# Another order of the six deep layers' queues, on all five engines of one core

## The reference

```
for i in range(DEPTH):                      # DEPTH = 6
    x = attn_layer(shift_tokens(x), Wqkv[i], q_scale[i], k_scale[i], Wo[i]) + x
    x = ffn_layer(shift_tokens(x), ln_g[i], ln_b[i], W1[i], b1[i], W2[i], b2[i]) + x
```

## Time and profile before

| | us |
|---|---|
| median of 3 runs (3456.48 to 3460.31) | 3459.82 |
| the profiled execution, its own time | 3457.47 |
| its span, first to last instruction | 3455.5 |
| TensorE busy | 3392.5 (98%) |
| VectorE busy | 3123.3 (90%) |
| ScalarE busy | 3047.1 (88%) |
| GpSimd busy | 2706.0 (78%) |

### The profile page before, as it was taken

How to read it: one execution, slowest core, us unless ns; L and a number is a source line. 1 busy time by engine, 2 the same in 40 slices (tenths; PEclk the granted TensorE clock), 3 DMA queues, 4 the chain that set the end, 5 groups by cost and what they waited for, 6 DMA issues and landing times.

```text
span 3455.5 us, 109160 instructions
## 1 busy us (share of the span) xinstructions
PE 3392.5 (98%) x43104; PEld 2518.0 (73%) x43104; DVE 3123.3 (90%) x4897; ACT 3047.1 (88%) x5393; POOL 2706.0 (78%) x2652
## 2 busy tenths in 40 slices
PE   8998899999999999999999999999999999999998
PEld 6885677777777777777777777777777777777776
DVE  6886999999999999999999999999999999989994
ACT  5665799999999999999999999999999999999996
POOL 3434888888888888888887888888888888888782
PEclk9998999999999999999999999999999999999999
DMA  1001212212211221221221221222122222122111
GB/s 44 27 3 46 56 39 58 68 39 53 55 49 48 68 52 40 55 58 39 67 52 43 52 58 47 59 52 52 43 58 55 51 52 52 38 74 52 37 50 42
DMA packets 61704, 171.33 MB, mean 50 GB/s; under 512 B 9488, under 2 KB 21392, under 8 KB 60816
## 3 DMA queue, kind: packets, MB, share of 16 engines
q1 hardware_dynamic: 61200, 164.36, 18.7%
HBM read 21.72 MB, written 4.19 MB: 8 GB/s over the span
## 4 chain that ended last, share of the span: by engine, by line
PE 88%; DVE 4%; DMA 3%; issue 2%; POOL 2%; ACT 1%; SPq 1%; DVEq 0%; POOLq 0%; ACTq 0%
PE bank L1021 11%; PE bank L1037 10%; PE bank L1002 9%; PE bank L969 9%; PE bank L986 8%; PE bank L1361 7%; PE bank L920 7%; PE bank L922 6%; PE bank L921 6%; PE bank L1374 3%; DMA vbuf<-v_stage 3%; PE bank L380 2%; PE bank L360 2%; PE bank L1346 2%; PE bank L345 2%
## 5 line engine op out<-in xcount | busy, mean ns | idle before, releaser
L1286 POOL TENSOR_TENSOR rotbuf<-mbuf 128x512 f32<-128x512 f32 x768 | 982.1, 1284 | 318.2 <-PE bank L969 308.5
L1300 POOL TENSOR_TENSOR rotbuf<-rotbuf,rs 128x512 f32<-128x512 f32 x768 | 793.8, 1044 | 7.5
L1173 DVE TENSOR_TENSOR mbuf<-bank,table 128x512 f32<-128x512 f32 x768 | 526.6, 686 | 100.4 <-ACT sq L1063 99.8
L1310 POOL TENSOR_TENSOR probs<-probs,rden 128x768 f32<-128x768 f32 x384 | 566.9, 1476 | 35.8 <-DVE rden L1252 28.5
L1063 ACT ACTIVATE sq<-bank 128x512 f32<-128x512 f32 x768 | 461.9, 601 | 71.0 <-PE bank L922 55.1
L1174 DVE TENSOR_TENSOR mbuf<-bank,table 128x512 f32<-128x512 f32 x768 | 522.3, 680 | 0.0
L969 PE MATMUL bank<-ident,rotbuf 128*128 128x128 f32 x3072 | 468.6, 275 | 7.7 <-DVE mbuf L1174 5.4
L969 PEld LDWEIGHTS bank<-ident,rotbuf 128*128 128x128 f32 x3072 | 365.9, 141 | 135.1 <-ACT qbuf L1083 18.1
L1155 DVE TENSOR_REDUCE ss<-sq 128x16 f32<-128x1024 f32 x384 | 461.3, 1201 | 0.2 <-issue 0.2
L920 PE MATMUL bank<-weights,inputs 128*128 128x512 bf16 x1152 | 444.6, 386 | 15.5 <-DVE mbuf L1174 11.8
L1021 PEld LDWEIGHTS bank<-probs_t,vbuf 96*64 96x64 f32 x12288 | 389.3, 138 | 96.3 <-issue 94.4
(11 more groups left out here) (115 smaller groups left out, 6269.2 us busy)
## 6 DMA issues: line engine op xcount, KB each, us to landing
vbuf<-v_stage SPq DMA_DIRECT2D x192, 384.0 KB, 4.5
vbuf<-v_stage SPq DMA_DIRECT2D x192, 256.0 KB, 3.5
vbuf<-v_stage SPq DMA_DIRECT2D x96, 128.0 KB, 4.5
stage<-in_wqkv SPq DMA_DIRECT2D x36, 256.0 KB, 5.0
weights<-in_wo SPq DMA_DIRECT2D x6, 512.0 KB, 6.3
out_t<-weights SPq DMA_DIRECT2D x1, 2048.0 KB, 6.3
weights<-out_t SPq DMA_DIRECT2D x1, 2048.0 KB, 10.6
out_t<-weights SPq DMA_DIRECT2D x16, 128.0 KB, 2.2
```

The costliest lines, as they stand in the source:

```text
L1173: e.tensor_tensor(b.m1[:, u % 2, :].rearrange("p (h s d) -> p h s d", h=8, s=2), pj, cos, ALU.mult)
L1286: e.tensor_tensor(b.rot[:, u, :], b.m1[:, u % 2, :], b.m2[:, u % 2, :], ALU.add).then_inc(s.rotated, 1)
L1300: e.tensor_tensor(v, v, r, ALU.mult).then_inc(s.scaled, 1)
L1310: e.tensor_tensor(probs, probs, b.rden[:, p % 2, :].unsqueeze(2).broadcast_to([P, 8, BLOCK_K]), ALU.mult).then_inc(s.probs, 1)
```

## The change

Nothing is computed differently and no step is added or dropped: each engine's slot holds the same steps in another order, many with another instance number, and the ring of the three shared banks follows TensorE's new order. The head of the diff:

```
 WORK_RING = (
-    ("up", 1, -3), ("pj", 5, 1), ("t", 4, 0), ("pj", 6, 1), ("up", 2, -3), ("t", 5, 0), ("t", 6, 0),
...
+    ("v", 2, 0), ("t", 0, 0), ("pj", 2, 1), ("out", 0, -2), ("t", 1, 0), ("t", 2, 0), ("pj", 3, 1),
+    ("up", 0, -3), ("t", 3, 0), ("up", 1, -3), ("v", 3, 0), ("up", 2, -3), ("pj", 4, 1), ("pj", 5, 1),
+    ("t", 4, 0), ("t", 5, 0), ("pj", 6, 1), ("mu", 0, -2), ("pj", 7, 1), ("dn", 0, -3), ("t", 6, 0),
+    ("t", 7, 0), ("v", 0, 1), ("v", 1, 1), ("pj", 0, 2), ("pj", 1, 2),
 )
 PE_REACH = (-3, 2)
-ACT_REACH = (-4, 2)
+ACT_REACH = (-3, 2)
 DVE_REACH = (-6, 2)
-POOL_REACH = (-2, 2)
-SP_REACH = (1, 1)
+POOL_REACH = (0, 2)
+SP_REACH = (0, 1)
```

```
+    act_copy_t(e, s, b, at, 1, 1)
+    act_ff_shift(e, s, b, at, -1)
+    act_square(e, s, b, at, 2, 3)
...
+    act_copy_t(e, s, b, at, 0, 2)
+    act_ff_gelu(e, s, b, at, -3, 0)
+    act_copy_pt_of(e, s, b, at, -1, 1)
+    act_copy_t(e, s, b, at, 0, 3)
+    act_ff_gelu(e, s, b, at, -3, 1)
     act_copy_v(e, s, b, at, 0, 3)
...
+    act_input_of(e, s, b, at, 2)
+    act_ff_gelu(e, s, b, at, -3, 2)
+    act_square(e, s, b, at, 1, 4)
+    act_mask(e, s, b, at, 0, 0)
+    act_square(e, s, b, at, 1, 5)
```

More of the change, by code:

```diff
@@ L1587, in pe_deep_slot @@
 def pe_deep_slot(e, s, b, at):
+    pe_transpose_probs_of(e, s, b, at, -1, 0)
+    pe_values_in(e, s, b, at, 0, 2)
+    pe_values_of(e, s, b, at, -2, 3)
+    pe_scores_of(e, s, b, at, -1, 2)
+    pe_transpose(e, s, b, at, 0, 0)
+    pe_project_in(e, s, b, at, 1, 2)
+    pe_project_out(e, s, b, at, -2)
+    pe_transpose(e, s, b, at, 0, 1)
+    pe_transpose(e, s, b, at, 0, 2)
+    pe_project_in(e, s, b, at, 1, 3)
+    pe_ff_up(e, s, b, at, -3, 0)
     pe_scores_of(e, s, b, at, -1, 3)
     pe_transpose_probs_of(e, s, b, at, -1, 1)
+    pe_transpose(e, s, b, at, 0, 3)
@@ L1699, in dve_deep_slot @@
     dve_shift(e, s, b, at, 0, 0)
+    dve_sum_squares(e, s, b, at, 1, 2)
+    dve_rope(e, s, b, at, 1, 6)
+    dve_ff_refine(e, s, b, at, -2)
     dve_rope(e, s, b, at, 1, 7)
[L1701 to L1707, removed]
     dve_ff_residual(e, s, b, at, -3)
@@ L1710, in dve_deep_slot @@
     dve_sum_of(e, s, b, at, 0, 0)
+    dve_sum_squares(e, s, b, at, 1, 3)
+    dve_clamp(e, s, b, at, 1)
+    dve_max_of(e, s, b, at, 0, 1)
+    dve_shift(e, s, b, at, 0, 1)
+    dve_rope(e, s, b, at, 2, 0)
+    dve_rope(e, s, b, at, 2, 1)
+    dve_max_of(e, s, b, at, 0, 2)
     dve_ff_norm(e, s, b, at, -2)
+    dve_shift(e, s, b, at, 0, 2)
     dve_sum_of(e, s, b, at, 0, 1)
+    dve_rope(e, s, b, at, 2, 2)
+    dve_residual_of(e, s, b, at, -1)
+    dve_sum_of(e, s, b, at, 0, 2)
     dve_sum_squares(e, s, b, at, 2, 0)
-    dve_rope(e, s, b, at, 2, 2)
@@ L1717, in pool_deep_slot @@
[L1717 to L1741 removed]
+    dve_rope(e, s, b, at, 2, 3)
@@ new lines, in dve_deep_slot @@
+    dve_max_of(e, s, b, at, 0, 3)
+    dve_ff_gate(e, s, b, at, -2, 0)
+    dve_shift(e, s, b, at, 0, 3)
+    dve_ff_gate(e, s, b, at, -2, 1)
+    dve_sum_squares(e, s, b, at, 2, 1)
+def pool_deep_slot(e, s, b, at):
+    pool_input_of(e, s, b, at, 2)
+    pool_rotate(e, s, b, at, 1, 6)
+    pool_normalise_of(e, s, b, at, 0, 0)
+    pool_rotate(e, s, b, at, 1, 7)
+    pool_refine(e, s, b, at, 1)
+    pool_scale(e, s, b, at, 1, 0)
+    pool_scale(e, s, b, at, 1, 1)
+    pool_rotate(e, s, b, at, 2, 0)
+    pool_scale(e, s, b, at, 1, 2)
+    pool_scale(e, s, b, at, 1, 3)
+    pool_normalise_of(e, s, b, at, 0, 1)
+    pool_rotate(e, s, b, at, 2, 1)
+    pool_rotate(e, s, b, at, 2, 2)
+    pool_normalise_of(e, s, b, at, 0, 2)
+    pool_scale(e, s, b, at, 1, 4)
+    pool_rotate(e, s, b, at, 2, 3)
+    pool_next_weights(e, s, b, at(0))
+    pool_scale(e, s, b, at, 1, 5)
+    pool_scale(e, s, b, at, 1, 6)
+    pool_scale(e, s, b, at, 1, 7)
+    pool_rotate(e, s, b, at, 2, 4)
+    pool_rotate(e, s, b, at, 2, 5)
+    pool_normalise_of(e, s, b, at, 0, 3)
```

129 lines of the change are left out of this document (46 added, 83 removed), and 3 rows, old and new, of the table WORK_RING.

## The result

The changed kernel takes 3544.28 us (median of 6 runs, 3541.4 to 3545.45), the one before 3459.20 in the same comparison: a ratio of 1.0244, 95% interval 1.0231 to 1.0257. It is slower by 85 us; 3519 was forecast, with a range of 3490 to 3560. The granted clock of the profiled execution is 0.995 of full speed, and 0.992 before, so the clock has no part in the loss.

The account below looks back on a forecast made before the run. TensorE was taken as the bound, 99.7% of the steady stretch being its own work. Slots of 31.8 + 1.0 = 32.8 against 32.11 gave 63.5 - 3 - 2 + 1, about 59 on 3457.5, plus 2.35 to the median: 3519 us, range 3490 to 3560.

Parts of the forecast that it names:

- cheaper neighbours: On TensorE, new block order: smaller start gaps bring a slot to 31.7 to 31.9; alone, 29 us less.
- the path that was named: From t1 over ScalarE and VectorE to pj6: 13.2 against TensorE's own 12.2, so 1.0 lost each slot.
- VectorE's wait at rope4: On VectorE, at the rotation of pj4: about 2 us idle a slot, waiting for the square behind the second load.
- the DMA wait: ScalarE's waits for the values' DMA, 76.2 us in all: would go, worth nothing as they lay under TensorE's work.
- Nothing else is late by more than a tenth: Rest of the slot: pj3 has 0.2 over the residual, v3 0.1 over gate0, GpSimd 0.5 in t0.
- more waits come on top: Rival: further waits outside t1 to pj6, or lengthening it; half a microsecond a slot, 46 more, 3565; chance 20%.
- the loop: Likeliest case: ScalarE and VectorE between t1 and pj6 make it slower, 3500 to 3541, slot 32.6 to 33.0; chance 70%.
- TensorE's own slot: TensorE's work in one new slot without waits: 31.7 to 31.9, taken as 31.8, against 32.11 before.
- the two switches from values to scores: On TensorE, two scores now behind values: 0.18 saved if free, at worst 0.09 extra each; cited weight-load rule favoured not free.
- Fill and drain: Time ahead of the first project-out and behind the last: -2 us, within -8 and +4.
- the first interval and the weight splitting: Outside the regular slots: 3 us less for a short first interval; weight splitting on GpSimd 0 to +3, taken as +1.
- the likeliest stretch: Whole time: 3500 to 3541, from slots of 32.6 to 33.0; chance 70%.

Follow-up runs that it names:

- e3: Changed kernel with VectorE's norm step directly behind the refine step, where GpSimd is idle: 3506.86 us, ratio 1.0135.
- e8: Changed kernel with only ScalarE's feed-forward shift moved, from ahead of the square of pj3 to behind the square of pj5: 3545.86 us, ratio 1.0254.
- e11: Changed kernel with VectorE's norm step one place earlier, ahead of the row maximum of s2: 3507.58 us, ratio 1.0135.
- e6: Kernel before the change with the identity in place of gelu, so without the two table loads a slot: 3442.07 us, ratio 0.9952.
- e10: e4 with the copy of t3 ahead of the copy of pt1 on ScalarE: 3417.37 us, ratio 0.9873.
- e4: Changed kernel with third gate ahead of pj4's rotation, input pair behind pj5's square, e3's move, outer sum at VectorE's slot end: 3435.71 us, ratio 0.9929.
- e5: Changed kernel with the identity in place of gelu, so without the two table loads a slot: 3437.05 us, ratio 0.9939.
- e7: e10 with ScalarE's feed-forward shift moved behind the square of pj5, as in e8: 3496.92 us, ratio 1.0110.

## Why the prediction was right, and where it was not

**The mechanism held.** TensorE had been nearly without a wait, so the new order had to win by cheaper neighbours or lose by waits. It lost by the path that was named, which runs through ScalarE without a gap and through rope4, gate2 and rope5, and comes back at pj6. s0, t4 and pj6 are late by 0.49, 0.18 and 0.28 in the changed kernel, where 0.3, 0.2 and 0.3 to 0.4 were named. VectorE's wait at rope4 is 2.14, where about 2 was named, and the DMA wait went. In e3 the path can be measured by itself and is 13.2, as summed.

**The step that failed is "Nothing else is late by more than a tenth".** t2 is late by 0.51. Its cause is VectorE's norm step, which the prediction carried at its old length. In the new order it starts under an instruction of GpSimd and takes 1.34 instead of 0.37. So the path from t1 to pj6 is 13.6 and not 13.2, and in the changed kernel it doesn't begin at t1's copy on ScalarE, but on VectorE, at the row maximum of s2, norm and rotation of pj2. The wait of 0.18 ahead of the square of pj3 shows this, and so does e8. e3 and e11, which change nothing but the place of this step, give 37 us back. The Trainium skill (SBUF — State Buffer, SBUF: two separate sides) says that VectorE, in an instruction with two SBUF inputs, and GpSimd, in one that reads SBUF, share a port pair as an exclusive lock, and that the one that starts second is blocked for the whole instruction. The rows agree: the step ends 0.27 and 0.28 after GpSimd's instruction. The held step could have been read from the trace of before, at 1.34 in its last layer. The rival "more waits come on top" is thus what happened, beside the loop and not in its place. It costs 0.43 a slot (33.03 against the 32.60 of e3), where the rival had half a microsecond.

**TensorE's own slot was mis-sized**: 31.8 was taken, and it is 31.4. About 0.1 of this is that the two switches from values to scores are free, which the prediction left open, with 31.7 for that case. The rule that was cited against them (the Trainium skill, TensorE: Matmul & The Clock Gate, Part 3, The mechanism), as the prediction applied it, is not borne out by the 1.08. The rest is that the 32.0 added up from the kernel before, called TensorE's own work, held waits too short for a bracket. Two of them are the 0.17 that e6 gives back. A third goes back to the wait for the values' DMA, which the prediction took to be worth nothing. ScalarE's rows first, then TensorE's:

```profile
1711.10 0.60 ACT L1095 ACTIVATE v_stage<-bank 128x512 f32<-128x512 f32 x1 [0.69 <-DMA vbuf<-v_stage]
```

```profile
1711.75 3.72 PE L1037 MATMUL bank<-outs_t,weights 128*128 128x256 f32 x16
```

The copy of values-in ends at 1711.70, and the project-out, which takes the bank that it frees, starts at 1711.75, 0.54 behind t2. Over the steady slots this distance is 0.57 (median), against 0.44 in the slots where project-out is in time, and a late project-out holds the next block back by another 0.10. No run took this wait away by itself, so what it cost is an estimate. By it TensorE's own slot before is 32.04 less 0.17, 0.13 and 0.10, about 31.6. The cheaper neighbours are worth 0.2 a slot, nearly all of it the two free switches. TensorE's own time from t1 to pj6 is 12.1 (12.40 in e10, less the 0.26). The loss that the 13.2 stands for is 1.1, and 31.4 + 1.1 + 0.1 (t6) is e3's slot of 32.60.

**The two errors partly cancel.** The slot is 31.4 + 1.6 = 33.0 instead of 31.8 + 1.0 = 32.8. That the forecast of 3519 lies only 25 us off is in part luck.

**The last layer was overlooked.** Its slots are 0.90 longer than the others (0.29 before), and 7 of them, with the 0.46 of the one before, make 7 us that no term of the sum held. Timeline of VectorE and of GpSimd in the last layer:

```profile
3189.83 1.49 DVE L1512 TENSOR_TENSOR weights<-weights,x_stream 128x256 f32<-128x256 f32 x1
```

```profile
3189.76 1.27 POOL L1286 TENSOR_TENSOR rotbuf<-mbuf 128x512 f32<-128x512 f32 x1 [2.68 <-PE bank L969]
```

The outer sum, an instruction of the last layer alone with both inputs in SBUF, starts 0.07 after a rotation's addition on GpSimd and ends 0.29 after it. It takes 1.49, against a median of 0.65 before. In these slots pt0 starts 1.24 behind the projection ahead of it instead of 0.65, waiting for GpSimd's softmax normalising. That the place of the outer sum is the cause was not tried by itself. e4 moved it together with three other steps, and there the last layer's slots are as short as the rest. In e5 it keeps its place but takes 0.42, and there they are as short, too.

**Fill and drain** were taken at -2 and are -2.9 ahead of the first project-out and +3.7 behind the 93rd, +0.8 in all. The table load has no drain behind it, as the prediction said: 1785.00 to 1786.30.

The sum once more, for the profiled executions: 87.0 in the slots and 0.8 outside them are 87.8, against the forecast's 59. Of the 29 that are missing 21 are the slot (0.23 over 91), 7 the last layer and 3 fill and drain; the first interval and the weight splitting take 2 off. The upper end of the likeliest stretch, 3541, does not follow from its slot of 33.0 either: 92 x 0.2 above 3519 is 3537. The 3544 measured lies in the range, but above that stretch.

## What to carry to other kernels

Where queues are in order and the work repeats in slots, take for each place where an engine waits the longest path that leaves the busy engine and comes back to it: a step costs nothing where its engine would wait for the busy one anyway (taking the shift out of such a stretch gained nothing in e8) and its whole length in a stretch that sets the slot (the same shift in e7). The busy shares don't tell the two apart. When an order is changed, durations change with it: a step of VectorE with two SBUF inputs has to be priced together with what GpSimd does at that moment, and steps that run only in one layer have to be followed in that layer. A busy engine's distances from block to block can hold short waits; the same distance in a slot or a run where nothing is late tells them from its own work. And when an order has lost by a few waits it pays to look at each of them: here four moved steps turned a loss of 85 us into a gain of 22, and a fifth into one of 42.

## What had not been expected of the hardware

The size of the coupling between VectorE and GpSimd: one and the same instruction took 0.37 us (median) in the kernel before, 0.42 with GpSimd idle in e3, 0.89 and 1.34 under GpSimd's instructions, each time to 0.27 or 0.28 after the end of GpSimd's instruction. It goes both ways: where both started within 0.03 us, in the kernel before, GpSimd's took 1.51 instead of 1.27. The rotations (L1173 and L1174, with one input in a PSUM bank) took 0.65 to 0.69 in all 1536 cases of the changed kernel, 855 of which started under an instruction of GpSimd. And scores behind values cost no more on TensorE (1.08) than a projection behind values, though each of them costs 0.09 at its start behind a block that uses all 128 rows.
